# A two-layer graph network on one core: layer 0 gathers normalised rows instead of products, each edge group once

## The chip, the core and the metric

The kernel runs on one core of a Trainium2 chip. The metric is the device time of one execution in microseconds. Before the change the median of three runs is 3737.38 us (3736.8 to 3738.64).

## The reference, cut to what matters

x is 6250 x 512. There are 100,000 edges, sorted by destination. Layer 0 is a mean over neighbours with two weight matrices, layer 1 an attention over the same edges.

```
h = relu(layernorm(x))
agg = segment_sum(h[src], dst);  deg = number of edges into each node
z = relu(agg / max(deg, 1) @ W_l.T + b_l + h @ W_r.T)
x = x + batch_norm(z, gamma, beta)          # mean and variance over the nodes
h = relu(layernorm(x))
K, Q, V = h @ Wk, h @ Wq, h @ Wv
e = exp(clip(K[src] . Q[dst] / 8, -5, 5))   # for each of 8 heads
x = x + batch_norm(h + segment_sum(V[src] * e, dst) / segment_sum(e, dst))
```

## The kernel before

The nodes are cut into 49 windows of 128 rows (the last has 106), the edges into 391 groups of 256 (`GROUPS`; a group is G = 2 gathers of 128 rows). A step pairs one group with one window. A group whose edges run into the next window has one more step there, so there are 391 + 48 = 439 steps, padded to 440 (`STEPS`), in a loop of 55 passes of U = 8 steps each. Which window a step belongs to depends on the edges, so `prepare` makes tables of it on the chip, one number for each step: `win_t` the window, `col_t` its column in the tile `sums`, `par_t` which half of the PSUM tiles it uses, `new_t` whether it is the first step of a window. An engine reads an entry into a register with `load_values` (L927, the load itself is at L929) or `value_load`, and `If` branches on it.

Layer 0 has these stages, one after the other, each closed by a barrier of all engines:

- `prepare`: the tables, and for each step the 256 source rows (`src_t`) and places in the window (`rel_t`).
- `embed`: the weights are scaled, transposed and split into two float16 parts; then for each window the layer norm h (ScalarE, L704), its transpose (TensorE, L772), its high part (ScalarE, L709) and low part (VectorE, L650) into `slots`, which is the tile `sums` seen as float16, the product y = h W_l.T (TensorE, L781, 12 matmuls), its two parts (L715, L654) and their store to `y_d` (SP, L588). x comes in blocks of four windows through two buffers (SP, L583).
- `aggregate`: GpSimd issues the gathers of the rows of `y_d`, two for a step (L831), unrolled; rows outside the step's window have an index over the bound and aren't fetched. VectorE makes for each step the matrix `hot` (L848), 1 where a gathered row belongs to a row of the window. TensorE adds hot times rows into `pss` and counts into `psc` (L921, L923). At the first step of a window it also clears these (L901, L902) and puts the product h W_r.T into `psz` (L905, 12 matmuls). When a window has ended, VectorE flushes it (`flush`, L852): divides, adds, applies relu, stores into `sums` and adds up S1 and S2.
- `coefficients`, and then `dense`, `attend` and the last batch norm, which make layer 1.

The order on each engine is the order of the code; no planner is at work. On TensorE's queue a step of the gather loop is L908 to L925: two table entries, one branch, two waits, six matmuls. Semaphores: `rows_in[u]` counts landed gathers, `hot_made` and `ps_made` count steps of VectorE and TensorE; GpSimd refills a buffer when `ps_made` says that it has been read (L828).

Of the kernel before, what the change touches and what calls it, by code (L numbers as in the profile page):

```python
# [16 lines left out]
F32 = mybir.dt.float32  # L17
# [7 lines left out]
ds = bass.ds  # L25
# [6 lines left out]
def build(nc, x, src, dst, W_l, b_l, W_r, gamma0, beta0, Wq, Wk, Wv, gamma1, beta1, out):  # L32
# [25 lines left out]
    y_d = nc.dram_tensor("y_d", (WINDOWS * P, 2 * D), F16).ap()  # L58
# [18 lines left out]
    with life:  # L77
# [10 lines left out]
        early = ExitStack()  # L88
        win_t = sb(early, "win_t", [1, TS], I16)

# [16 lines left out]
        def prepare():  # L107
            with ExitStack() as ctx:
                fill = sb(ctx, "fill", [1, 2, TAIL], I32)
# [23 lines left out]
                ps_t = [pb(ctx, f"ps_t{k}", [P, 512]) for k in range(2)]  # L133

                filled, padded, got_first = sem("filled"), sem("padded"), sem("got_first")
# [7 lines left out]
                def _(block):  # L143
                    @block.sync
                    def _(sp):
                        sp.dma_start(first_i[:, :], dst[:].rearrange("(a e) -> a e", a=1)[:, 0:E:GE],
                                     allow_slow_non_contiguous=True).then_inc(got_first, 16)
                        for pad, given in ((src_pad, src), (dst_pad, dst)):
                            flat = pad.rearrange("a b -> (a b)")
                            sp.dma_start(flat[0:E].rearrange("(a b) -> a b", a=16),  # L150
                                         given[:].rearrange("(a b) -> a b", a=16)).then_inc(padded, 16)
                        sp.wait_ge(filled, 2)
                        for k, pad in enumerate((src_pad, dst_pad)):
                            flat = pad.rearrange("a b -> (a b)")
                            sp.dma_start(flat[E:E + TAIL].rearrange("(a b) -> a b", a=1),
                                         fill[:, k, :]).then_inc(padded, 16)

# [24 lines left out]
                    def _(pe):  # L182
# [11 lines left out]
                        last.then_inc(cols_ps, 1)  # L194
                        for n, (table, c) in enumerate((t, c) for t in range(2) for c in range(TCH)):
# [8 lines left out]
                            last.then_inc(turned, 1)  # L204

                    @block.vector
                    def _(dve):
# [33 lines left out]


# [9 lines left out]
                        for n, (table, c) in enumerate((t, c) for t in range(2) for c in range(TCH)):  # L252
# [3 lines left out]
                                                  ps_t[n % 2][:, 0:GE].rearrange("p (g s) -> p g s", g=G)).then_inc(stored, 1)  # L256

# [275 lines left out]
        def embed(w_r16, bias, unscale):  # L533

            with ExitStack() as ctx:
                w_l16 = sb(ctx, "w_l16", [P, 2, KC, D], F16)
                w_raw = sb(ctx, "w_raw", [P, 2, KC, D])
                big = sb(ctx, "big", [P, 2, KC])  # L540
                top = sb(ctx, "top", [P, KC])
                base2 = sb(ctx, "base2", [P, KC], I32)
                grow = sb(ctx, "grow", [P, KC])
                diag = sb(ctx, "diag", [P, KC, P])
                b_row = sb(ctx, "b_row", [1, D])
# [7 lines left out]
                y16 = sb(ctx, "y16", [P, 2, 2, D], F16)  # L553
                ps_w = [pb(ctx, f"ps_w{k}", [P, 512]) for k in range(2)]
                ps_u = pb(ctx, "ps_u", [P, 512])
                ps_b = pb(ctx, "ps_b0", [P, 512])
                ps_t = [pb(ctx, f"ps_t0{k}", [P, 512]) for k in range(2)]
                ps_o = [pb(ctx, f"ps_o0{k}", [P, 512]) for k in range(2)]
                w_in, b_in, x_in, stored = sems("w_in0", 2), sem("b_in0"), sems("x_in0", 2), sems("stored0", 2)
                chain, grown, w_scaled, w_turned, w_high, w_split, spread, unscaled = (  # L560
                    sem(n + "0") for n in ("wchain", "grown", "w_scaled", "w_turned", "w_high", "w_split", "spread", "unscaled"))
                counted, joined, var_ready, dev_ready, scale_ready, shift_ready = (
                    sem(n + "0") for n in ("counted", "joined", "var_ready", "dev_ready", "scale_ready", "shift_ready"))
                h_made, turned, high, split, made, y_high, y_low = (
                    sem(n + "0") for n in ("h_made", "turned", "high", "split", "made", "y_high", "y_low"))
                slots = sums[:, :].bitcast(F16)
                w16 = (w_l16, w_r16)
                assert FOURS % 2 == 0

                def slot(w, part):  # L570
                    return slots[:, ds(w * 2 * WIDTH + part * D, D)]
# [5 lines left out]
                def _(block):  # L577
                    @block.sync
                    def _(sp):
# [10 lines left out]
                        for k, w in enumerate((W_l, W_r)):  # L590
                            sp.dma_start(w_raw[:, k, :, :], w[:, :].rearrange("(c p) i -> p c i", p=P)).then_inc(w_in[k], 16)
                        load(0, 0)
                        sp.dma_start(b_row[:, :], b_l[:].rearrange("(a n) -> a n", a=1)).then_inc(b_in, 16)
                        load(1, 1)
                        with sp.Fori(0, FOURS // 2 - 1) as i:
                            for half in range(2):
                                for b in range(NB):
                                    store(NB * (2 * i + half) + b, b % 2)
                                load(2 * i + half + 2, half)
                        for b in range(NB):  # L600
                            store(NB * (FOURS - 2) + b, b % 2)
                        sp.wait_ge(h_made, NB * (FOURS - 1))
                        sp.dma_start(x_sb[0:LAST, 0, 0, :], x[(WINDOWS - 1) * P:N, :]).then_inc(x_in[0], 16)
                        for b in range(NB):
                            store(NB * (FOURS - 1) + b, b % 2)
                        store(WINDOWS - 1, 0)
                        for par in range(2):
# [822 lines left out]
```

## Time and profile before

| | |
|---|---|
| profiled execution | 3740.36 us |
| its span | 3738.0 us |
| median of the runs | 3737.38 us |
| `prepare`, from 0 us | 43.4 us |
| `embed`, from 43.4 us | 272.2 us |
| `aggregate`, from 315.6 us | 1174.4 us |
| the rest, from 1490 us | 2248.0 us |
| VectorE, TensorE, GpSimd busy in the span | 67%, 81%, 53% |

The stages don't overlap, so the span is the sum of the four, and what a change to one of them is worth shows in that stage alone. A queue's own instructions (register, branch, table entry) are not in an engine's busy time; the view by source line lists them with the letter q behind the engine: PEldq is TensorE's queue.

### The profile page before, as it was taken

What the parts mean: (1) busy time and instruction counts of PE and PEld (TensorE: products, weight loads), DVE (VectorE), ACT (ScalarE), POOL (GpSimd) and SP (SyncE); (2) the same over time, 40 slices, a digit from 0 to 9 for tenths busy, and PEclk for the clock granted to TensorE, in tenths of its full rate; (3) what the DMA queues carried; (4) which work ended last, traced back from release to release, by engine and by line L of the source; (5) the groups of instructions that cost most, each with busy time, mean ns of one, the idle gap of its engine ahead of it and who ended that gap; (6) DMA issues with size and microseconds to landing.
All of it is one profiled execution on the core that took longest, in us unless ns stands there. A gap on an engine that the chain in (4) does not pass through costs nothing. (4 is left out here: it accounts for less than half of the span.)

```text
span 3738.0 us, 59649 instructions
## 1 busy us (share of the span) xinstructions
PE 3025.4 (81%) x11648; PEld 1516.3 (41%) x11649; DVE 2503.8 (67%) x4615; ACT 1632.8 (44%) x6216; POOL 1991.4 (53%) x1929
## 2 busy tenths in 40 slices
PE   4776777777777776599998999999999999999640
PEld 2332222222222222488884444444444444444210
DVE  4444333333333333555557999999999999999999
ACT  2331000000000000222226999999999999999410
POOL 1004777777777776111115555555555555555455
PEclk9887766667776767799998999999999999999865
DMA  2334666666666665344446888887888888888337
GB/s 71 110 109 133 176 176 175 177 175 180 176 175 174 176 175 153 113 143 151 147 145 245 276 277 277 278 275 270 274 276 276 276 276 277 277 276 277 104 116 218
DMA packets 263476, 750.48 MB, mean 201 GB/s; under 512 B 54179, under 2 KB 54181, under 8 KB 263402
## 3 DMA queue, kind: packets, MB, share of 16 engines
q0 software_dynamic: 197504, 615.66, 52.1%
q1 hardware_dynamic: 58910, 121.60, 10.1%
q10 hardware_dynamic: 7020, 12.80, 0.9%
q14 instruction: 33, 0.27, 0.0%
q8 instruction: 9, 0.15, 0.0%
HBM read 750.45 MB, written 77.83 MB: 222 GB/s over the span
## 5 line engine op out<-in xcount | busy, mean ns | idle before, releaser
L1080 POOL DMA_INDIRECT kv<-kv_d,src_t x880 | 876.9, 997 | 633.4 <-PE psw L1226 464.1
L831 POOL DMA_INDIRECT rows<-y_d,src_t x880 | 898.0, 1020 | 555.8 <-DVE rows L838 288.1
L1102 ACT ACTIVATE kv<-kv,wgt 128x64 f32<-128x64 f32 x4400 | 1096.8, 334 | 0.0
L1223 PE MATMUL psa<-kv,hot 128*128 128x512 f32 x1760 | 863.6, 613 | 29.1 <-ACT kv L1102 27.7
L921 PE MATMUL pss<-rows,hot 128*128 128x512 f16 x1760 | 632.5, 494 | 273.4 <-DMA rows<-y_d,src_t 238.0
L1132 DVE TENSOR_TENSOR kv<-kv,ps_q 128x1024 f32<-128x1024 f32 x440 | 533.0, 1211 | 32.6 <-PE ps_q L1207 24.0
L1145 DVE TENSOR_REDUCE score<-kv 128x16 f32<-128x1024 f32 x440 | 531.2, 1207 | 0.0
L1019 ACT ACTIVATE var<-var 128x512 f32<-128x512 f32 x2 | 1.3, 629 | 1187.7 <-DVE var L1006 1187.7
L1223 PEld LDWEIGHTS psa<-kv,hot 128*128 128x128 f32 x1760 | 304.1, 190 | 395.9 <-issue 387.1
L1207 PE MATMUL ps_q<-sums,hotT 128*128 x1760 | 454.4, 381 | 0.1
L855 DVE TENSOR_SCALAR rd<-psc 128x1 f32 (+1 forms) x49 | 7.7, 158 | 599.7 <-PE psc L923 599.7
L921 PEld LDWEIGHTS pss<-rows,hot 128*128 128x128 f16 x1760 | 126.3, 109 | 497.5 <-issue 450.9
L1226 PE MATMUL psw<-parts,hot 128*128 128x16 f32 x880 | 302.2, 415 | 0.0
L848 DVE TENSOR_TENSOR hot<-lane,rel_t 128x256 f16<-128x256 f32 x440 | 187.9, 428 | 155.6 <-issue 97.2
L351 POOL TENSOR_TENSOR x_sb<-x_sb,C_bc 128x512 f32<-128x512 f32 x49 | 63.5, 1296 | 409.1 <-DMA x_sb<-in_x 409.1
L1226 PEld LDWEIGHTS psw<-parts,hot 128*128 128x128 f32 x880 | 167.8, 191 | 210.7 <-issue 210.7
L1138 DVE TENSOR_TENSOR kv<-kv,wgt 128x384 f32<-128x384 f32 x440 | 240.9, 547 | 0.3 <-ACT wgt L1095 0.3
L517 PE MATMUL ps_o<-w_hi,hT_hi 128*128 128x512 f32 x588 | 236.4, 402 | 0.0
L517 PE MATMUL ps_o<-w_lo,hT_hi 128*128 128x512 f32 x588 | 235.3, 400 | 0.0
L517 PE MATMUL ps_o<-w_hi,hT_lo 128*128 128x512 f32 x588 | 231.2, 393 | 0.0
L1207 PEld LDWEIGHTS ps_q<-sums,hotT 128*128 128x128 f16 x1760 | 172.4, 98 | 110.5 <-issue 2.0
L1198 PE MATMUL ps_h<-ident,hot 128*128 128x128 f32 x880 | 193.3, 302 | 14.9 <-DVE hot L1124 14.4
(191 smaller groups left out, 3620.1 us busy)
## 6 DMA issues: line engine op xcount, KB each, us to landing
kv_d<-o_sb SPq DMA_DIRECT2D x49, 512.0 KB, 2.8
rows<-y_d,src_t POOLq DMA_INDIRECT x880, 3.7
kv<-kv_d,src_t POOLq DMA_INDIRECT x880, 5.3
y_d<-y SPq DMA_DIRECT2D x49, 256.0 KB, 2.0
x_d<-x_sb SPq DMA_DIRECT2D x49, 256.0 KB, 3.2
h_d<-h SPq DMA_DIRECT2D x49, 256.0 KB, 3.4
h1b<-h_d SPq DMA_DIRECT2D x49, 256.0 KB, 2.7
x1b<-x_d SPq DMA_DIRECT2D x49, 256.0 KB, 4.0
```

What stands on the lines that cost most here:

```text
L517: last = nc.tensor.matmul(ps_o[par][k][:, :], a, b[:, k, c, :], start=(c == 0 and j == 0), stop=(c == KC - 1 and j == 2))
L831: pool.indirect_dma_start(rows[:, u, g, :], None, y_d[0:N, :], bass.IndirectOffsetOnAxis(src_t[:, m:m + 1], 0), bounds_check=limit, oob_is ...
L921: nc.tensor.matmul(pss[:, ds(par, D)], hot[:, u, g, :], rows[:, u, g, part * D:(part + 1) * D], start=False, stop=(g == G - 1 and part == ...
L1080: pool.indirect_dma_start(kv[:, u, g, :], None, kv_d[0:N, :], bass.IndirectOffsetOnAxis(src_t[:, m:m + 1], 0), bounds_check=limit, oob_is_ ...
L1102: last = nc.scalar.mul(v, v, wgt[:, u, g * HEADS + h:g * HEADS + h + 1])
L1132: nc.vector.tensor_tensor(k, k, ps_q[u % 2][:, :].rearrange("p (g d) -> p g d", g=G), ALU.mult).then_inc(multiplied, 1)
L1138: nc.vector.tensor_tensor(v, v, w.unsqueeze(3).to_broadcast([P, G, HEADS - HA, DH]), ALU.mult)
L1145: nc.vector.tensor_reduce(score[:, u, :].rearrange("p (g h) -> p g h", g=G), kv[:, u, :, 0:D].rearrange("p g (h d) -> p g h d", h=HEADS), ...
L1198: last = nc.tensor.transpose(ps_h[:, g * P:(g + 1) * P], hot[:, u, g, :].bitcast(F32), ident[:, :])
L1207: last = nc.tensor.matmul(ps_q[u % 2][:, g * D:(g + 1) * D], hotT[:, u % 2, g * P:(g + 1) * P], slots[:, ds(col * 2 + k * D, D)], start=(k ...
L1223: nc.tensor.matmul(pss[:, ds(par, D)], hot[:, u, g, :].bitcast(F32), kv[:, u, g, D:2 * D], start=False, stop=(g == G - 1), skip_group_chec ...
L1226: last = nc.tensor.matmul(psc[:, 0:2 * HEADS], hot[:, u, g, :], parts[:, u % 4, g, :, :].rearrange("p t h -> p (t h)"), start=False, stop= ...
```

## The change

- `embed` makes only h, and splits it without a transpose (ScalarE's high part straight from `h`, VectorE's low part too). TensorE has nothing to do there. The two parts are stored from `slots` to a tensor `h0_d` of the same shape as `y_d`. The next block of x is asked for after the third store of a block instead of the fourth. The work on the weights moves to `prepare`.
- `prepare` makes seven more tables (`end_t`, `done_t`, `past_t`, `prev_t`, `need_t`, `ring_t` for each step, `last_t` for each group) and the source rows in natural order, `nat_t`.
- In `aggregate` the gathers go by group, not by step: 391 x 2, without a bound, into a ring of 8 groups. TensorE reads from the tables where in the ring a step's group lies (`ring_t`) and how many groups must have landed (`need_t`). SP hands the landings on to TensorE (`ready`) and the buffers back to GpSimd (`free`).
- The sums in `pss` are now of h. After a window has ended, VectorE and ScalarE make its mean in two float16 parts (`average`, `turn_over`); TensorE transposes h (`turn_h`, in the next step), the mean (`turn_mean`, one step later) and makes both products (`multiply`, 24 matmuls, two steps later); VectorE flushes the window when the one after it ends. Before every step TensorE's queue tests for each of the three whether it is due.

```diff
+    then(nc.vector.memset(end_t[:, :], 0))
+    then(nc.vector.memset(done_t[:, 0:2], 0))
+    then(nc.vector.tensor_scalar(done_t[:, 2:TS + 2], win[:, :], -1.0, 0.0, ALU.add, ALU.max))
+    then(nc.vector.tensor_copy(end_t[:, 3:TS + 2], new_t[:, 1:TS]))
+    then(nc.vector.scalar_tensor_tensor(past_t[:, :], win[:, :], 2.0, new_t[:, :], ALU.is_ge, ALU.mult))
+    then(nc.vector.tensor_scalar(prev_t[:, :], win[:, :], -2.0, 0.0, ALU.add, ALU.max))
+    then(nc.vector.tensor_scalar(slot_i[:, :], grp[:, :], 0.0, float(GROUPS - 1), ALU.max, ALU.min))
+    then(nc.vector.tensor_scalar(need_t[:, :], slot_i[:, :], 1.0, None, ALU.add))
+    then(nc.vector.tensor_scalar(slot_i[:, :], slot_i[:, :], U - 1, None, ALU.bitwise_and))
+    then(nc.vector.tensor_scalar(ring_t[:, :], slot_i[:, :], float(G * 2 * D), None, ALU.mult))
+    dve.wait_ge(summed_g, 1)
+    then(nc.vector.scalar_tensor_tensor(last_t[:, 0:GROUPS], step[0:1, 0:GROUPS], float(U + 1), ps_g[0:1, 0:GROUPS],
+                                        ALU.add, ALU.add))
...
+        nc.vector.tensor_copy(nat_t[:, c * P:c * P + n], ps_t[c % 2][:, 0:n]).then_inc(stored, 1)
...
-    def store(w, par):
-        sp.wait_ge(y_high, w + 1)
-        sp.wait_ge(y_low, w + 1)
-        sp.dma_start(y_d[ds(w * P, P), :], y16[:, par, :, :].rearrange("p a d -> p (a d)")).then_inc(stored[par], 16)
+    def store(w):
+        sp.wait_ge(split, w + 1)
+        sp.dma_start(h0_d[ds(w * P, P), :], slot(w, 0, 2)).then_inc(stored, 16)
...
-            load(2 * i + half + 2, half)
+                    load(2 * i + half + 2, half)
...
+        nc.vector.tensor_tensor(slot(w, 1), h[:, b % 2, :], slot(w, 0), ALU.subtract).then_inc(split, 1)
...
+        act.wait_ge(h_made, w + 1)
+        nc.scalar.copy(slot(w, 0), h[:, b % 2, :]).then_inc(high, 1)
...
-    def products(w, par):
-        pe.wait_ge(split, w + 1)
-        if not below(w, 2):
-            pe.wait_ge(y_low, w - 1)
-        for c in range(KC):
-            for part, of in ((0, 0), (0, 1), (1, 0)):
-                last = nc.tensor.matmul(ps_o[par][:, :], slots[:, ds(w * 2 * WIDTH + part * D + c * P, P)], w_l16[:, of, c, :],
-                                        start=(c == 0 and part == of == 0), stop=(c == KC - 1 and part == 1))
...
-    limit = pool.alloc_register("limit0")
-    pool.reg_mov(limit, N - 1)
-    for s in range(STEPS):
-        u = s % U
-        if s < U:
-            pool.wait_ge(cleared, u + 1)
-        pool.wait_ge(ps_made, s + 1)
+    for n in range(GROUPS):
+        if n >= U:
+            pool.wait_ge(free, n - U + 1)
         for g in range(G):
-            m = s * G + g
-            pool.indirect_dma_start(rows[:, u, g, :], None, y_d[0:N, :],
-                                    bass.IndirectOffsetOnAxis(src_t[:, m:m + 1], 0),
-                                    bounds_check=limit, oob_is_err=False).then_inc(rows_in[u], 16)
+            pool.indirect_dma_start(at_ring(n % U, g), None, h0_d[0:N, :],
+                                    bass.IndirectOffsetOnAxis(nat_t[:, n * G + g:n * G + g + 1], 0)).then_inc(rows_in[n % U], 16)
+@block.sync
...
+    def pass_on(n, i, u, release=True):
+        sp.wait_ge(rows_in[u], 16 * G * (i + 1))
+        sp.sem_inc(ready, 1)
+        if release:
+            last = sp.value_load(last_t[0:1, ds(n - LAG, 1)], min_val=1, max_val=U + STEPS)
+            sp.wait_ge(ps_made, last)
+            sp.sem_inc(free, 1)
...
+    def turn_over(w, par):
+        act.wait_ge(rd_ready, w + 1)
+        nc.scalar.mul(mean[:, 0, :], pss[:, par * D:(par + 1) * D], rd[:, 0:1]).then_inc(mean_high, 1)
+        act.wait_ge(h_turned, w + 1)
+        act.wait_ge(products, w + 1)
+        for part in range(2):
+            last = nc.scalar.copy(hT[:, part, :], ps_x[part][:, :])
+        last.then_inc(h_copied, 1)
+        act.wait_ge(m_turned, w + 1)
+        for part in range(2):
+            last = nc.scalar.copy(mT[:, part, :], ps_x[part][:, :])
+        last.then_inc(m_copied, 1)
...
+    def average(w, par):
+        nc.vector.tensor_scalar(rd[:, :], psc[:, ds(par, 1)], 1.0, None, ALU.max).then_inc(counted, 1)
+        dve.wait_ge(counted, w + 1)
+        nc.vector.reciprocal(rd[:, :], rd[:, :]).then_inc(rd_ready, 1)
+        dve.wait_ge(mean_high, w + 1)
+        nc.vector.scalar_tensor_tensor(mean[:, 1, :], pss[:, ds(par, D)], rd[:, 0:1], mean[:, 0, :],
+                                       ALU.mult, ALU.subtract).then_inc(mean_split, 1)
...
+    def flush(w, n=P):
         base = w * IN_FLUSH
-        nc.vector.tensor_scalar(rd[:, :], psc[:, ds(par, 1)], 1.0, None, ALU.max).then_inc(flushing, 1)
+        to, kept = sums[:, ds(w * WIDTH, D)], sums[0:n, ds(w * WIDTH, D)]
+        dve.wait_ge(products, w + 2)
...
+    def close_before(s):
+        [ended] = load_values(mybir.EngineType.DVE, end_t, s + 2, 1, 1)
+        with dve.If(ended):
+            w = dve.value_load(win_t[0:1, ds(s - 1, 1)], min_val=0, max_val=WINDOWS - 1)
             [par] = load_values(mybir.EngineType.DVE, par_t, s - 1, 1, D)
-            w = dve.value_load(win_t[0:1, ds(s - 1, 1)], min_val=0, max_val=WINDOWS - 1)
+            [past] = load_values(mybir.EngineType.DVE, past_t, s, 1, 1)
+            with dve.If(past):
+                flush(dve.value_load(prev_t[0:1, ds(s, 1)], min_val=0, max_val=WINDOWS - 2))
             dve.wait_ge(ps_made, s + U)
             alone(dve)
-            flush(w, at, par)
...
-    def open_window(w, at, par):
-        pe.wait_ge(flushed, w + 1)
+    pe.sem_inc(products, 1)
+    pe.wait_ge(const, 2)
+    def turn(parts, count):
+        for part in range(2):
+            for c in range(KC):
+                last = nc.tensor.matmul(ps_x[part][:, c * P:(c + 1) * P], parts(part, c), ident16[:, :], start=True, stop=True)
+        last.then_inc(count, 1)
+    def turn_h(w):
+        pe.wait_ge(m_copied, w + 1)
+        turn(lambda part, c: slots[:, ds(w * 2 * WIDTH + part * D + c * P, P)], h_turned)
+    def turn_mean(w):
+        pe.wait_ge(h_copied, w + 1)
+        pe.wait_ge(mean_split, w + 3)
+        turn(lambda part, c: mean[:, part, c * P:(c + 1) * P], m_turned)
+    def multiply(w):
+        pe.wait_ge(m_copied, w + 2)
+        pe.wait_ge(taken, w + 1)
+        for k, (given, weights) in enumerate(((hT, w_r16), (mT, w_l16))):
+            for c in range(KC):
+                for part, of in ((0, 0), (0, 1), (1, 0)):
+                    last = nc.tensor.matmul(ps_z[:, :], given[:, part, c * P:(c + 1) * P], weights[:, of, c, :],
+                                            start=(k == c == part == of == 0), stop=(k == 1 and c == KC - 1 and part == 1))
+        last.then_inc(products, 1)
+    def of_window(s):
+        return pe.value_load(done_t[0:1, ds(s + 2, 1)], min_val=0, max_val=WINDOWS - 1)
+    def open_window(s, par):
+        w = pe.value_load(win_t[0:1, ds(s, 1)], min_val=0, max_val=WINDOWS - 1)
+        pe.wait_ge(mean_split, w + 1)
         nc.tensor.matmul(pss[:, ds(par, D)], zero[0:1, 0:P], zero[0:1, :], start=True, stop=False, skip_group_check=True)
         nc.tensor.matmul(psc[:, ds(par, 2)], zero[0:1, 0:P], zero[0:1, 0:2], start=True, stop=False, skip_group_check=True)
-        for c in range(KC):
-            for part, of in ((0, 0), (0, 1), (1, 0)):
-                nc.tensor.matmul(psz[:, ds(par, D)], slots[:, ds(at * 2 + part * D + c * P, P)], w_r16[:, of, c, :],
-                                 start=(c == 0 and part == of == 0), stop=(c == KC - 1 and part == 1), skip_group_check=True)
+    def after(s, lag, what):
+        [ended] = load_values(mybir.EngineType.PE, end_t, s - lag + 2, 1, 1)
+        with pe.If(ended):
+            what(of_window(s - lag))
     with pe.Fori(0, ITERS) as i:
         for u in range(U):
             s = i * U + u
+            after(s, 2, multiply)
+            after(s, 1, turn_mean)
+            after(s, 0, turn_h)
             [par] = load_values(mybir.EngineType.PE, par_t, s, 1, D)
             [new] = load_values(mybir.EngineType.PE, new_t, s, 1, 1)
+            [ring] = load_values(mybir.EngineType.PE, ring_t, s, 1, (U - 1) * G * 2 * D)
+            need = pe.value_load(need_t[0:1, ds(s, 1)], min_val=1, max_val=GROUPS)
             with pe.If(new):
-                [at] = load_values(mybir.EngineType.PE, col_t, s, 1, (WINDOWS - 1) * WIDTH)
-                w = pe.value_load(win_t[0:1, ds(s, 1)], min_val=0, max_val=WINDOWS - 1)
-                open_window(w, at, par)
+                open_window(s, par)
             pe.wait_ge(hot_made, s + 1)
-            pe.wait_ge(rows_in[u], (i + 1) * 16 * G)
+            pe.wait_ge(ready, need)
             for g in range(G):
                 for part in range(2):
-                    nc.tensor.matmul(pss[:, ds(par, D)], hot[:, u, g, :], rows[:, u, g, part * D:(part + 1) * D],
+                    nc.tensor.matmul(pss[:, ds(par, D)], hot[:, u, g, :], rows[:, ds(ring + (g * 2 + part) * D, D)],
                                      start=False, stop=(g == G - 1 and part == 1), skip_group_check=True)
                 last = nc.tensor.matmul(psc[:, ds(par, 2)], hot[:, u, g, :], ones16[:, :],
                                         start=False, stop=(g == G - 1), skip_group_check=True)
             last.then_inc(ps_made, 1)
+    after(STEPS, 2, multiply)
```

How the instructions stand, first TensorE's queue in the gather loop before the change, from the matmuls of one step to the branch of the next (L921 and L923 are matmuls, the lines at L929 load a table entry, L913 jumps over the opening of a window):

```order
L921 ISA
L921 MATMUL pss<-rows,hot 128x512 x2
L923 REGISTER_ALU
L923 MATMUL psc<-ones,hot 128x2
L921 MATMUL pss<-rows,hot 128x512 x2
L923 MATMUL psc<-ones,hot 128x2
L929 ISA
L929 TENSOR_LOAD par_t
L929 REGISTER_ALU
L929 TENSOR_LOAD new_t
L913 COMPARE_AND_BRANCH
```

Of the same place after the change, the first of the three tests ahead of a step, with what it jumps over (L1006 loads the entry, L973 is the branch, L958 the products):

```order
L994 MATMUL psc<-ones,hot 128x2
L1006 TENSOR_LOAD end_t
L973 COMPARE_AND_BRANCH
L963 REGISTER_ALU
L963 TENSOR_LOAD done_t
L963 ISA x2
L953 REGISTER_ALU
L954 REGISTER_ALU
L958 MATMUL ps_z<-w_r,hT 128x512 x12
L958 MATMUL ps_z<-w_l,mT 128x512 x12
L973 UNCONDITIONAL_BRANCH
```

It is followed by two more of this kind and then by the step's own four entries and the branch at L986 over the opening of a window (L1006 and L985 are entries, L992 the step's matmuls):

```order
L1006 REGISTER_ALU
L1006 TENSOR_LOAD par_t
L1006 REGISTER_ALU
L1006 TENSOR_LOAD new_t
L1006 REGISTER_ALU
L1006 TENSOR_LOAD ring_t
L985 REGISTER_ALU
L985 TENSOR_LOAD need_t
L985 ISA x2
L986 COMPARE_AND_BRANCH
```

The step's two entries have become four, three tests with an entry and a branch of their own stand ahead of them, and the 12 matmuls that stood in the opening have become 24 behind the first test.

GpSimd's queue from `prepare` to the end of `aggregate`, before:

```order
L177 DMA eidx<-dst_pad,grp_col 128x256
L102 UNCONDITIONAL_BRANCH
L820 UNCONDITIONAL_BRANCH
L831 DMA rows<-y_d,src_t 128x1024 x880
L102 UNCONDITIONAL_BRANCH
```

and after:

```order
L227 DMA eidx<-dst_pad,grp_col 128x256
L112 UNCONDITIONAL_BRANCH
L815 UNCONDITIONAL_BRANCH
L821 DMA rows<-h_d,nat_t 128x1024 x782
L112 UNCONDITIONAL_BRANCH
```

The gathers have become 782 instead of 880, and stand in the same place.

## Rows read from the trace of the kernel before

**Rows 1.** Stretches: length; PE, PEld, DVE, ACT, POOL busy (count); PEclk; DMA share; GB/s.
```profile
0.00:43.40 43.40, 11.98 (x36) 6.89 (x37) 17.37 (x47) 0.00 (x0) 10.11 (x21) 1.00 0.14 43
43.40:315.60 272.20, 188.03 (x826) 93.49 (x826) 125.40 (x257) 103.11 (x178) 0.00 (x0) 0.90 0.29 102
315.60:1490.00 1174.40, 858.84 (x3326) 325.55 (x3326) 395.11 (x843) 0.00 (x0) 898.02 (x880) 0.70 0.62 175
1490.00:3738.00 2248.00, 1966.58 (x7460) 1090.41 (x7460) 1965.95 (x3469) 1529.71 (x6038) 1083.23 (x1028) 0.94 0.69 229
```

**Rows 2.** Line L831, its instructions, its idle time, its landings.
```profile
L831 POOL DMA_INDIRECT rows<-y_d,src_t x880: 994/998/1520, 316.8 to 1481.8; - x176
...
  PE psc L923: 6.1, 20
...
DMA to landing us min/median/max: 2.1/3.7/4.4
```

**Rows 3.** Timeline near 1431 us: start, us, engine, line, tiles, idle before.
```profile
1430.52 1.00 POOL L831 DMA_INDIRECT rows<-y_d,src_t  x1 [0.30 <-issue]
...
1431.82 1.00 POOL L831 DMA_INDIRECT rows<-y_d,src_t  x1 [0.30 <-issue]
...
1433.29 1.03 PE L921 MATMUL pss<-rows,hot 128*128 128x512 f16 x2 [1.81 <-DMA rows<-y_d,src_t]
...
1434.19 1.01 PE L921 MATMUL pss<-rows,hot 128*128 128x512 f16 x2
```

**Rows 4.** PE queue, by source line: ns min/median/max, first and last start.
```profile
L929 PEldq ALU_OP  x489: 32/32/36, 316.3 to 1482.9; - x163
...
L929 PEldq TENSOR_LOAD <-par_t x440: 282/287/480, 315.8 to 1482.6; - x147
...
L929 PEldq FUSED_REGOPS  x385: 37/37/42, 326.0 to 1482.5; - x193
...
L913 PEldq COMPARE_BRANCH  x440: 66/207/369, 316.8 to 1483.4; - x147
...
L915 PEldq FUSED_REGOPS  x49: 151/151/168, 317.8 to 1466.2; - x49
...
L915 PEldq SEQ_ASSERT  x49: 18/18/32, 318.0 to 1466.4; - x49
...
L908 PEldq COMPARE_BRANCH  x55: 76/208/208, 340.7 to 1484.4; - x55
```

**Rows 5.** The same view of 1414.45 to 1420.4 us.
```profile
L929 PEldq FUSED_REGOPS  x3: 37/37/42, 1414.5 to 1420.2; - x3
...
L905 PEldq FUSED_REGOPS  x8: 46/46/65, 1417.0 to 1418.0; - x8
```

**Rows 6.** The page, DMA queues: packets, MB, share of 16 engines.
```profile
q14 instruction: 33, 0.27, 0.0%
```

**Rows 7.** Timeline of one block of four windows in `embed`.
```profile
220.45 0.69 DVE L632 BATCH_NORM_STATS2 st<-x_sb 128x6 f32<-128x512 f32 x1 [5.80 <-DMA x_sb<-in_x]
...
222.88 0.68 DVE L650 TENSOR_TENSOR sums<-ps_t,sums 128x512 f32 x1
...
229.72 0.58 ACT L709 CAST sums<-ps_t 128x512 f32 x1 [0.36 <-PE ps_t L772]
...
230.20 0.82 ACT L704 ACTIVATE h<-x_sb,nb,rs 128x512 f32<-128x512 f32 x1
...
234.31 0.41 SPq L583 DMA_DIRECT2D x_sb<-in_x  x1
...
239.99 0.69 DVE L632 BATCH_NORM_STATS2 st<-x_sb 128x6 f32<-128x512 f32 x1 [5.70 <-DMA x_sb<-in_x]
```

**Rows 8.** Timeline of `prepare` and of the weights.
```profile
31.29 0.35 DVE L245 TENSOR_SCALAR rel<-eidx,win_col 128x256 f32<-128x256 int32 x1 [13.11 <-DMA eidx<-dst_pad,grp_col]
...
49.05 2.29 DVE L621 TENSOR_REDUCE big<-w_raw 128x4 f32<-128x2048 f32 x1 [5.87 <-DMA w_raw<-in_L_gnn_W_l]
...
78.08 0.69 DVE L670 TENSOR_TENSOR bias<-bias,ps_b 128x512 f32<-128x512 f32 x1
```

More of the change, by code:

```diff
@@ L606, in _ @@
-                        store(WINDOWS - 1, 0)
-                        for par in range(2):
-                            sp.wait_ge(stored[par], 16 * (PAIRS + 1 - par))
+                            store(NB * (FOURS - 1) + b)
+                        store(WINDOWS - 1)
+                        sp.wait_ge(stored, 16 * WINDOWS)
                     @block.vector
                     def _(dve):
-                        done = [0]
-                        def then(ins):
-                            done[0] += 1
-                            ins.then_inc(chain, 1)
-                            dve.wait_ge(chain, done[0])
@@ new lines, in _ @@
+                    @block.sync
+                    def _(sp):
+                        LAG = U // 2
+                        def pass_on(n, i, u, release=True):
[5 more added lines that the diff above has]
+                                sp.sem_inc(free, 1)
+                        for u in range(U):
+                            pass_on(u, 0, u, u >= LAG)
+                        with sp.Fori(1, GROUPS // U) as i:
+                            for u in range(U):
+                                pass_on(i * U + u, i, u)
+                        for n in range(GROUPS // U * U, GROUPS):
+                            pass_on(n, n // U, n % U)
@@ new lines, in _ @@
+                    @block.scalar
+                    def _(act):
+                        act.sem_inc(m_copied, 1)
+                        nc.scalar.copy(ident16[:, :], ident[:, :]).then_inc(const, 1)
+                        def turn_over(w, par):
[10 more added lines that the diff above has]
+                            last.then_inc(m_copied, 1)
+                        with act.Fori(0, PAIRS) as i:
+                            for par in range(2):
+                                turn_over(2 * i + par, par)
+                        turn_over(WINDOWS - 1, 0)
@@ L925, in _ @@
                                 last.then_inc(ps_made, 1)
+                        after(STEPS, 2, multiply)
+                        after(STEPS, 1, turn_mean)
+                        after(STEPS + 1, 2, multiply)
+                        turn_h(WINDOWS - 1)
+                        turn_mean(WINDOWS - 1)
+                        multiply(WINDOWS - 1)
         def load_values(engine, table, s, n, most):
```

346 lines of the change are left out of this document (166 added, 180 removed).

## Prediction

> **What bounds the kernel now.** I read the stretches first. The stages follow one another, and the change touches the first three: 43.4, 272.2 and 1174.4 us [rows 1]. The 2248 us behind them keep their code and are carried over.
>
> In `aggregate` I then read the line of the gathers. The 880 gathers of L831 start from 316.8 to 1481.8 us, so one every 1.325 us, where one takes 0.998, and GpSimd waited for TensorE only 6.1 us in all [rows 2]. The timeline shows the same: 1.30 us from one gather to the next with 0.30 of issue between them, and TensorE waiting 1.81 us for rows to land [rows 3]. So GpSimd's queue sets the pace, 2.65 us for a step of two gathers. TensorE follows it at a mean granted clock of 0.70 with 859 us busy [rows 1].
>
> The third view is TensorE's own queue, which the busy time doesn't count. An entry of a table takes 0.287 us in it, a branch that jumps 0.207 us [rows 4], and a step has two entries and one branch. That this queue works one instruction after the other, also while the array is busy, is seen in 1414.5 to 1420.2 us: the three L929 instructions there enclose an opening of a window and one more step, without a wait for a landing [rows 5]. Counted off the listing these are 35 instructions. By the medians of [rows 4, 5] (four entries in the opening step and two in the other, 1.72; two branches, 0.28; the long L915 and its assert, 0.17; L905's eight, 0.39; the 17 others at 0.03 to 0.05, 0.63) they take 3.19 us; the stretch is 5.7 us. So behind each stand 0.07 us more, part of it for the 52 matmuls and weight loads pushed on the way. For the new step I take 0.065.
>
> In `embed` a block of four windows goes round in 19.5 us, from one landing of x (220.45) to the next (239.99): 13.9 us until the next load is issued at 234.31, and 5.7 until it lands [rows 7].
>
> **The change, part by part.** First the gathers. 782 at 1.325 are 1036 us instead of 1166, 130 less. What the bound check costs no row shows; at most the 0.33 us around the gather's own 0.998, so 780 to 1036, and I take 1036, the row of the same gather. This is worth something only as long as GpSimd sets the pace.
>
> TensorE's queue, ordinary step. In front of the step stand three entries and three branches that jump, then four entries, a long register instruction with its assert, and the branch over the opening; the six matmuls now need four address instructions, since the ring's place is a register. That makes 23 instructions: 7 entries at 0.286 (2.00), 4 jumps at 0.207 (0.83), 5 at 0.032 (0.16), 5 at 0.040 (0.20), 0.151 + 0.018 (0.17), sum 3.36; behind them 23 x 0.065 = 1.50. So 4.86 us, against 2.65 of the gathers. Even the recorded durations alone, 3.36, are longer than two gathers. 440 steps take 2138 us. The loop's end is a jump of 0.208 and two short ones, 0.5 us, 55 times: 27 us.
>
> The window's work. In 49 windows each of the four branches falls through once (0.07 instead of 0.21: -0.53) and each body loads one more number (0.032 + 0.286 + 0.151 + 0.018 + 4 x 0.065 = 0.75, four times 3.0). The other register instructions are seven short ones and nine for addresses, 1.7; pushing 80 more matmuls and weight loads I put at 0.2. So 4.4 us, 216 us in all.
>
> What lies beside it. TensorE's array has for two groups at the low clock 1.8 us (0.90 from one to the next [rows 3]), well below 4.86. The 24 matmuls of `multiply` take at most 24 x 0.45 = 10.8 us and are pushed in one go, while the queue reads the entries of the next two steps (9.7 us): hidden, at 1 to 5 us a window if not, 0 to 250 us; I take 0. VectorE's 395 us and ScalarE's three new copies and one scaling (about 0.6 us each by L709 [rows 7], five passes, 3 us of a window's 44) are beside it as well. The new waits: `turn_mean` stands one step, 4.9 us, behind the end of the window, and its mean is ready after about 2.5 us (two short VectorE instructions, under 0.35 each by L245 [rows 8], a ScalarE pass of 0.58 and a VectorE pass of 0.68 [rows 7], and their hand-overs); `multiply` one step later again. Behind a waiting instruction stand the next matmuls, and GpSimd waits behind those, but with 1.5 us or less of cover used up in 4.9, I take 0; with every wait a full 2.3 us it is 113. SP loads one entry for a group, 0.3 us of some 6: nothing.
>
> Ends of the stage: the first rows land 6 us after its start; behind the last step now stand the transposes, the mean, 24 matmuls at the low clock and the flush, 18 us. Sum of `aggregate`: 2138 + 27 + 216 + 24 = 2405 us instead of 1174.
>
> `embed` loses its products, so its round is the chain from landing to load. After a landing VectorE has two statistics (0.69 us, 0.9 with what joins them) and the low part of the first window (0.68); that frees ScalarE for the third (0.82 and 0.58); for the fourth it waits behind the square root until the fourth statistics, 5.4 us, and is done at 6.3. Then the load is issued and takes 5.7: 12.0 us for the round instead of 19.5. 12 rounds and 8 us of ends are 152 us instead of 272. With stores in the load's way up to 1 us more a round: 152 to 165.
>
> `prepare` takes over the weights, 49.05 to 78.77 us [rows 8], 29.7 us; it hides 13.1 us of them in the wait for `eidx` [rows 8]; the seven tables are 12 instructions of 512 numbers or fewer (0.4 us each, L245 has 0.35: 5 us), the natural order seven small transposes with their copies (I put 0.7 on each: 5 us). 43.4 + 29.7 - 13.1 + 10 = 70 us, 62 to 80.
>
> **The sum.** 70 + 152 + 2405 + 2248 = 4875 us of span, with the 2.4 us around it 4877; the profiled execution lay 3 us over the median, so 4874. I say 4870.
>
> **The rivals.**
>
> *GpSimd stays the bound* (faster). If the queue's entries were hidden behind the array, the stage would be 782 x 1.325 plus 30, 1066, and the time 70 + 152 + 1066 + 2248, 3539 us. For it: TensorE is 27% idle in this stage [rows 1]. Against: the steps of [rows 5] run at the queue's pace with the array full.
>
> *The array binds.* At the low clock 440 steps of 1.8, and 49 windows with 24 matmuls at 0.45, 16 transposes at about 0.12 and the opening's 1 us, are 792 + 672, 1464 us: 3940 us. This needs the queue to be hidden too, and a clock that doesn't rise under full load.
>
> *The loop's code is fetched anew in every pass.* The body grows from 530 to about 1240 instructions. If every piece of 128 (8 KB) cost 2 us when it is fetched, ten of them in 55 passes, 1100 us more: 5970. Against: only 33 pieces in the whole span [rows 6], with loop bodies of 500. The skill gives TensorE an instruction cache of 128 KB, four times that of the other engines (same page, ISA Cache), which would hold 1240 of 64 bytes; no run here shows it.
>
> *A jump costs no more than a branch that falls through.* The long ones of [rows 4] could be waits of another kind. At 0.07 (the minimum there) instead of 0.207 the four jumps of a step save 0.55 us, 241 us: 4630. Against: the median of 440 is the long one, 391 of them do jump. The Trainium skill speaks for less as well: "Advanced Engine Details and Errata", Control Flow Timing, states about 108 ns for a compare-and-branch; this trace doesn't agree (0.207), and by the page it would be about 4700 us.
>
> *The hand-overs at a window's end bite* (slower still): a wait of 2.3 us in the window and an unhidden `multiply` of 5 us, 7.3 x 49, 360 us: 5230.
>
> **How the numbers follow.** The forecast 0.77 (its own range 4650 to 5080: 4.4 to 5.3 us for a step), the hand-overs 0.07, the cheap jump 0.03, the refetch 0.04, GpSimd 0.04, the array 0.03, something else 0.02. My range leaves out the last five and takes in the unhidden `multiply` in part: 4650 to 5120. What a measurement can tell from no change is 0.2%, 7.5 us. Only the GpSimd case is faster, nothing that I can name lands within 0.2%, so 0.04, 0.01 and 0.95.
>
> **What would show it.** Right: in `aggregate` a step every 4.9 us, TensorE's seven entries and four branches following each other without a gap, an idle array with "issue" as its releaser, GpSimd waiting for SP, the DMA share at about half, granted clock mostly at the low level (0.5, 1.2 GHz); `embed` with a round of 12 us. Wrong: gathers at 1.3 us from one another, or waits of TensorE's queue for `ready`, `mean_split` or `m_copied`. A step under 4.4 us or over 5.3 means that the price of an entry, a jump, or of the gap behind them is not what I read.

## The result, and the profile after

The changed kernel takes 5060.86 us (median of 4 runs, 5059.87 to 5061.24), the kernel before 3738.01 us (4 runs, 3736.8 to 3742.25): a ratio of 1.3531, 95% interval 1.3514 to 1.3548. The forecast was 4870, in a range of 4650 to 5120. The direction and the mechanism came as said; the time is 190 us over the number.

The stretches of the profiled execution, cut at the same four places as before (columns as in [rows 1]):

```profile
0.00:65.40 65.40, 26.86 (x87) 16.78 (x88) 41.09 (x90) 10.76 (x17) 10.11 (x21) 0.86 0.21 67
65.40:233.40 168.00, 0.00 (x0) 0.00 (x0) 78.19 (x186) 71.45 (x112) 0.00 (x0) 0.50 0.45 153
233.40:2812.20 2578.80, 1250.59 (x4698) 518.36 (x4699) 387.50 (x835) 139.18 (x246) 758.12 (x782) 0.58 0.29 80
2812.20:5059.10 2246.90, 1961.12 (x7460) 1089.82 (x7460) 1969.16 (x3468) 1529.80 (x6038) 1086.81 (x1028) 0.95 0.68 230
```

`prepare` and `embed` together went from 316 to 233 us, `aggregate` from 1174 to 2579, and the rest stayed where it was. In `aggregate` the DMA share fell from 0.62 [rows 1] to 0.29, and the array is busy for less than half of the stretch.

The gathers, which set the pace before [rows 2], by their line (durations in ns, then idle time and how often):

```profile
L821 POOL DMA_INDIRECT rows<-h_d,nat_t x782: 940/946/1437, 234.2 to 2740.6; - x196
...
  SPq L834: 1625.3, 378
  POOLq L112: 205.3, 1
  issue: 123.9, 403
...
DMA to landing us min/median/max: 3.2/3.5/5.8
```

GpSimd now waits 1625 us for SP, which gives a place in the ring back only when TensorE has read it. Each gather is 52 ns shorter than with the bound (0.946 instead of 0.998), and that is worth nothing here.

The timeline of one ordinary step, where [rows 3] had TensorE waiting for rows:

```profile
1309.99 0.25 PEld L992 LDWEIGHTS pss<-rows,hot 128*128 128x128 f16 x2 [4.17 <-issue]
1310.00 1.03 PE L992 MATMUL pss<-rows,hot 128*128 x2 [3.69 <-issue]
...
1311.71 0.21 PE L994 MATMUL psc<-ones,hot 128*128 128x2 f16 x1
1312.23 0.94 POOL L821 DMA_INDIRECT rows<-h_d,nat_t  x1 [3.41 <-SPq L834]
1313.48 0.95 POOL L821 DMA_INDIRECT rows<-h_d,nat_t  x1 [0.30 <-issue]
1315.02 0.23 PEld L992 LDWEIGHTS pss<-rows,hot 128*128 128x128 f16 x2 [3.59 <-issue]
1315.03 1.03 PE L992 MATMUL pss<-rows,hot 128*128 x2 [3.11 <-issue]
```

From 1309.99 to 1315.02 is one step, 5.03 us, of which the array works 1.9 and then stands idle for 3.11 with "issue" as the releaser: nothing that the profile calls a wait. What fills that time is only in the view of the queue by source line (ns min/median/max, first and last start):

```profile
L1006 PEldq TENSOR_LOAD <-end_t x1323: 282/287/477, 234.2 to 2796.1; - x189
L1006 PEldq TENSOR_LOAD <-ring_t x440: 282/284/298, 237.6 to 2792.4; - x147
...
L985 PEldq TENSOR_LOAD <-need_t x440: 282/283/303, 238.1 to 2792.9; - x147
L985 PEldq FUSED_REGOPS  x440: 151/151/166, 238.4 to 2793.2; - x147
...
L973 PEldq COMPARE_BRANCH  x1323: 63/200/350, 234.7 to 2796.4; - x189
...
L986 PEldq COMPARE_BRANCH  x440: 75/207/217, 238.7 to 2793.5; - x147
...
L989 PEldq EVENT_SEMAPHORE  x440: 51/51/51, 240.0 to 2793.8; - x147
```

A step has seven entries and four branches, at the prices of [rows 4]. They follow one another with about 0.06 us between the end of one and the start of the next, 0.08 where matmuls are handed over in between. Of the 12,334 gaps of the stage 50 are over 1 us, and 48 of these stand behind L954 (below). Over the 439 distances between the L985 entries of one step and the next the shortest is 4.97 and the median 5.03 us.

### The profile page after: what moved, and what is told of

Same layout as the page of the kernel before. It is cut to its first block and busy times, and to the rows that moved or that the text cites. A ratio compares the mean times of both kernels' runs of the same rounds, so it can differ in the third digit from the quotient of the medians.

```text
span 5059.1 us, 70485 instructions
## 1 busy us (share of the span) xinstructions
PE 3238.6 (64%) x12245; PEld 1625.0 (32%) x12246; DVE 2475.9 (49%) x4579; ACT 1751.2 (35%) x6413; POOL 1855.0 (37%) x1831
## 5 line engine op out<-in xcount | busy, mean ns | idle before, releaser
L821 POOL DMA_INDIRECT rows<-h_d,nat_t x782 | 758.1, 969 | 1954.5 <-SPq L834 1625.3
L992 PE MATMUL pss<-rows,hot 128*128 x1760 | 776.6, 575 | 1083.3 <-issue 1020.4
L851 ACT ACTIVATE mean<-pss,rd 128x512 f16<-128x512 f32 x49 | 33.7, 687 | 2085.5 <-DVE rd L886 2085.5
L992 PEld LDWEIGHTS pss<-rows,hot 128*128 128x128 f16 x1760 | 161.6, 113 | 1367.9 <-issue 1343.4
L968 PE MATMUL pss<-zero 1*128 1x512 f32 x49 | 38.4, 784 | 311.7 <-issue 311.7
L958 PE MATMUL ps_z<-w_r,hT 128*128 128x512 f16 x588 | 207.7, 527 | 12.2 <-issue 10.3
```

Of the source, the lines that this page charges most:

```text
L821: pool.indirect_dma_start(at_ring(n % U, g), None, h0_d[0:N, :], bass.IndirectOffsetOnAxis(nat_t[:, n * G + g:n * G + g + 1], 0)).then_inc ...
L958: last = nc.tensor.matmul(ps_z[:, :], given[:, part, c * P:(c + 1) * P], weights[:, of, c, :], start=(k == c == part == of == 0), stop=(k ...
L992: nc.tensor.matmul(pss[:, ds(par, D)], hot[:, u, g, :], rows[:, ds(ring + (g * 2 + part) * D, D)], start=False, stop=(g == G - 1 and part ...
```

## The experiments

All are compared with the kernel before on the same chip. Stages are cut as above.

**Entries alone, not used.** In every step of the kernel before, ahead of its branch over the opening:

```diff
+    for _ in range(3):
+        load_values(mybir.EngineType.PE, nil_t, s, 1, 1)
```

> The kernel before, with three more table entries read by TensorE's queue in every step (values not used). My theory (the queue works one instruction after the other and is hidden only up to GpSimd's 2.65 us): an entry with the address instruction ahead of it takes 0.34 + 0.09 us, so 3 x 0.437 x 440 = 577 us more on the queue, whose own work without waits was 823 us in the stage; 1400 plus some 15 of ends, 1415 instead of 1174: 3980 us in all, with GpSimd waiting for TensorE. Rival (entries are hidden behind the array or prefetched): no change, 3740.

Measured 3741.17 us against 3740.79, ratio 1.0 (0.999 to 1.0009). This says nothing on either theory: the trace has no entry of `nil_t` on TensorE's queue, since a value that nobody reads is left out when the program is made. It shows only how well two programs agree that differ by one cleared table.

**Entries and jumps.**

```diff
+    for _ in range(3):
+        [nil] = load_values(mybir.EngineType.PE, nil_t, s, 1, 1)
+        with pe.If(nil):
+            pe.sem_inc(never, 1)
```

> The kernel before, with three more entries in every step and behind each a branch that always jumps (the table is all zero). My theory: each pair costs 0.437 + 0.265 us, 927 us more on the queue, stage 1765 us, 4330 in all, 350 over the run with the entries alone. Rival (a jump costs what a branch that falls through costs, 0.13 with its gap): 174 over the run with the entries alone, 4155. Rival (hidden): 3740.

Measured 4267.56 us (ratio 1.1403, 1.1384 to 1.1422). Its queue and its gathers:

```profile
L918 PEldq COMPARE_BRANCH  x1320: 200/200/337, 318.8 to 2012.3; - x189
...
L936 PEldq TENSOR_LOAD <-nil_t x1320: 281/283/324, 318.4 to 2012.0; - x189
...
L834 POOL DMA_INDIRECT rows<-y_d,src_t x880: 992/998/1231, 318.3 to 1985.6; - x176
...
  PE psc L930: 609.8, 305
```

GpSimd, which had waited 6.1 us for TensorE [rows 2], now waits 609.8. A step takes 3.51 us (median). Before it took 1.57 where nothing was waited for (the shortest distances between two L913 branches, 50 of 439 under 1.75 us), so 1.94 more: 3 x (0.344 + 0.259) with the gaps, and one address instruction of 0.093 for all three, where I had put one on each: that accounts for the 62 us by which the forecast was high. Entries hidden behind the array (3740) are out. Jumps at 0.13 would have made 3.1 us a step, so the cheap jump is out too.

**Entries that are used, and no jumps.**

```diff
+    nil = [load_values(mybir.EngineType.PE, nil_t, s, 1, 1)[0] for _ in range(6)]
+    count_at = sum(nil, par)
...
-    last = nc.tensor.matmul(psc[:, ds(par, 2)], hot[:, u, g, :], ones16[:, :],
+    last = nc.tensor.matmul(psc[:, ds(count_at, 2)], hot[:, u, g, :], ones16[:, :],
```

> The kernel before, with six more table entries (all zero) read by TensorE's queue in every step, and this time their sum goes into the address of the counts' matmuls, so that they can't be left out. No jumps. My theory: a step's queue had 1.57 us where nothing waited, and gets 6 x 0.344 + 0.09 us and about 0.1 for the sum: 3.8 us, over GpSimd's 2.65; with 118 us for the windows and 27 for the loop's ends 1817 us instead of 1174, 4380 in all. With the jumps' run (3.51 us a step) a jump is then worth 0.27 us with its gap. Rival (an entry is hidden, only jumps cost): 3740. Rival (an entry costs what a short register instruction does, 0.09): 3740 too, since the step stays at 2.2 us.

Measured 4443.04 us (ratio 1.1878, 1.1858 to 1.1898), 63 over the forecast.

```profile
L933 PEldq TENSOR_LOAD <-nil_t x2640: 281/288/310, 319.1 to 2188.5; - x189
...
L927 PEldq FUSED_REGOPS  x440: 175/175/186, 328.0 to 2189.4; - x147
```

A step takes 3.93 us (3.8 expected), 2.36 more: 6 x 0.346, 0.093, and 0.14 for the longer address instruction of L927, and 0.05 over that sum. An entry is thus paid in full, and from the run before 1.94 - 0.093 - 3 x 0.344 leaves three jumps at 0.27 us each with their gaps. The rival of a cheap jump had 0.13 with its gap.

**One test ahead of the three.** The changed kernel with a table `due_t`, the largest of the three entries that are tested:

```diff
+    [due] = load_values(mybir.EngineType.PE, due_t, s, 1, 1)
+    with pe.If(due):
+        after(s, 2, multiply)
+        after(s, 1, turn_mean)
+        after(s, 0, turn_h)
-    after(s, 2, multiply)
-    after(s, 1, turn_mean)
-    after(s, 0, turn_h)
```

> The changed kernel with one test more ahead of the three (a table that says whether any of them is due), so that an ordinary step has five entries and two jumps instead of seven and four. My theory (the number of queue instructions sets the step): 1.40 us less in some 293 steps, 0.57 more in some 147: ordinary step 3.6 us instead of 5.0, 326 us less, 4735. Rival (it is the fetching of the loop's code, which grows here): no less than 5060. Rival (hand-overs at a window's end make the rest): less than 200 us won.

Measured 4859.12 us (ratio 1.2985, 1.2963 to 1.3007), 202 under the changed kernel's 5060.86: more than nothing, which refutes the fetch, but 124 less than I had said. It is also hardly more than the 200 that the rival of the hand-overs allowed, so by its total alone this run doesn't tell that rival from the queue; the steps do. An ordinary step takes 3.92 us and not 3.6: two entries and two jumps went (1.22 us), but one more register instruction came (0.10), since the wait is now computed on its own, and none of the tests' address instructions went, since the three tests had shared one. A step in which h or the mean is turned went up from 6.74 to 7.64 us, 0.9 instead of 0.57, because values that were read ahead of the branch are made anew behind it.

**Eight matmuls for a window instead of 24.** The 16 matmuls that have a low part in them are left out:

```diff
-    for part, of in ((0, 0), (0, 1), (1, 0)):
-        last = nc.tensor.matmul(ps_z[:, :], given[:, part, c * P:(c + 1) * P], weights[:, of, c, :],
+    last = nc.tensor.matmul(ps_z[:, :], given[:, 0, c * P:(c + 1) * P], weights[:, 0, c, :],
...
```

> The changed kernel with 8 instead of 24 matmuls in the products of a window (only high part times high part; the other 16 are left out). The trace shows 2.61 us between the last register instruction ahead of these matmuls and the next entry. Theory A (each of the 48 matmuls and weight loads takes 0.054 us to hand over): 0.9 us instead of 2.6, 85 us less, 4975. Theory B (handing over is cheap, the queue to the array is full and waits for it): 0.1 to 0.25 us, 112 to 120 us less, 4945. Rival (the gap is a fetch of code, which is there whatever the matmuls are): no less than 5050, the gap stays at 2 us or more.

Measured 4947.54 us (ratio 1.3221, 1.3199 to 1.3243), 113 less. In the changed kernel the last register instruction ahead of the products and the first entry behind them stand like this (the view of the queue, 344.5 to 348.5 us, for the entry to 347.6):

```profile
L954 PEldq ALU_OP  x1: 32/32/32, 344.8 to 344.8; - x1
...
L1006 PEldq TENSOR_LOAD <-end_t x1: 286/286/286, 347.5 to 347.5; - x1
```

and in this kernel at the same kind of place:

```profile
L954 PEldq ALU_OP  x1: 32/32/32, 292.7 to 292.7; - x1
...
L1005 PEldq TENSOR_LOAD <-end_t x2: 283/285/287, 292.8 to 293.5; - x2
```

The median gap over all 48 windows is 2.61 us in the one and 0.08 in the other; the mean is 2.45 in the changed kernel, and 48 x (2.45 - 0.08) is 114 us, the whole difference. Theory A, 0.054 us for each matmul and load, would have left 0.9 us here; so 8 matmuls and 8 weight loads are handed over for next to nothing, and with 24 and 24 the queue stands. Theory B, that it waits until the array has taken some, is the one that fits, and the trace of the changed kernel shows how many (the timeline, 344.5 to 348.5 us):

```profile
344.93 0.13 PEld L958 LDWEIGHTS ps_z<-w_r,hT 128*128 128x128 f16 x2 [1.16 <-issue]
...
347.04 0.15 PEld L958 LDWEIGHTS ps_z<-w_r,hT 128*128 128x128 f16 x1 [0.28 <-issue]
347.47 0.15 PEld L958 LDWEIGHTS ps_z<-w_r,hT 128*128 128x128 f16 x1 [0.28 <-issue]
347.83 0.74 PEld L958 LDWEIGHTS ps_z<-w_r,hT 128*128 128x128 f16 x4 [0.21 <-issue]
```

When the next entry starts, at 347.49, the array has begun 8 of the 24 loads and 7 of the 24 matmuls, and 33 of the 48 lie handed over and not begun. It is 8 and 7 in all 48 windows, and the same in the four other runs that have these 24 matmuls; only the time that the array takes for them differs (1.86 to 2.61 us here). With 8 and 8 at most 16 are handed over at this place.

The page's instruction line is the same in both kernels, and in all the kernels with the new stage:

```profile
q14 instruction: 297, 2.43, 0.2%
```

264 pieces more than [rows 6] do come, but their number doesn't move when TensorE's loop loses 256 instructions (this run) or more, and no gap of TensorE's queue is left that they could explain. In the changed kernel they come with the windows and not with the passes of TensorE's loop: from 12 us before to 2 us behind each L954 the DMA packets have five of them in 41 of 48 cases. Whose code they are no run shows.

**By step instead of natural order.** The changed kernel with this part undone: `ring_t`, `need_t` and SP's handing on go, the 880 gathers with a bound come back.

```diff
-    [ring] = load_values(mybir.EngineType.PE, ring_t, s, 1, (U - 1) * G * 2 * D)
-    need = pe.value_load(need_t[0:1, ds(s, 1)], min_val=1, max_val=GROUPS)
...
-    pe.wait_ge(ready, need)
+    pe.wait_ge(rows_in[u], (i + 1) * 16 * G)
```

> The changed kernel with the gathers of the kernel before in place of the natural order: 880 by step, with a bound, each step its own place; the entries for the place in the ring and for the count of groups go, and SP hands nothing on. The three tests and the rest of the change stay. My theory (the queue's instructions): five entries, four jumps and seven short ones, 3.4 us a step instead of 5.03, still over GpSimd's 2.65: 440 x 3.4 + 320 for the windows + 27 + 18 of ends, 1860 us for the stage, 4340 in all, so the natural order cost some 700 us of the 1320. Rival (the natural order was worth its 130 us on GpSimd): over 5060. Rival (only the tests' jumps count): 4900 or more.

Measured 4348.2 us (ratio 1.1625, 1.1606 to 1.1644); a step takes 3.44 us. So the natural order, whose own row promised 130 us, costs 713: two entries, the asserted load's long register instruction with its assert, three address instructions for places that are no longer fixed, and two short ones, nine of 24 instructions and 1.58 us of a step.

```profile
L826 POOL DMA_INDIRECT rows<-h_d,src_t x880: 992/997/1462, 237.0 to 2051.3; - x176
...
  PE psc L980: 772.0, 383
```

GpSimd still waits 772 us for TensorE, this time because of the tests.

**All look-ups in one number, gathers by step.** Half of the sums and three flags in one 16-bit entry; the work at a window's end stays as changed.

```diff
+    [v] = load_values(mybir.EngineType.PE, pack_t, s, 1, D + 7)
+    par = v & D
+    with pe.If(v & 7):
+        with pe.If(v & 4):
+            multiply(of_window(s - 2))
+        with pe.If(v & 2):
+            turn_mean(of_window(s - 1))
+        with pe.If(v & 1):
+            w = of_window(s)
+            turn_h(w)
+            open_window(w + 1, par)
```

> The changed kernel with the gathers of the kernel before (880, by step, with a bound, each with its own place, so neither a place in the ring nor a count of groups is looked up) and with half of the sums and the three tests in one number for each step: one entry, one jump over everything that a window's end needs. New embed and both products at the window's end stay. Theory A (the queue's time is the sum of its instructions): by the slots of the runs so far an ordinary step is 1.33 us of queue, a window's work 9.0 us more, 1053 us in all, under GpSimd's 1166; GpSimd sets the pace again: 65 + 168 + 1190 + 2247 = 3670 us, 2% faster than before. Rival (the array binds: at the low clock a window of nine steps has 16.2 + 10.2 + 3 = 29 us of matmuls against 23.8 of gathers): 49 x 29.4 = 1440, 3920 us. Between them, if the clock rises for a part of the time as before: 3700 to 3800.

Measured 3668.19 us (5 runs, 3665.63 to 3670.21; ratio 0.9806, 0.9793 to 0.982): 1.9% under the kernel before, and as forecast (3670). Its `embed` and `aggregate`, columns as above:

```profile
61.50:232.60 171.10, 2.67 (x11) 1.19 (x9) 81.19 (x193) 71.75 (x113) 0.00 (x0) 1.00 0.45 150
232.60:1419.30 1186.70, 945.70 (x4698) 431.22 (x4698) 396.04 (x843) 138.36 (x245) 898.89 (x880) 0.83 0.63 175
```

and its gathers, by their line:

```profile
L814 POOL DMA_INDIRECT rows<-h_d,src_t x880: 994/999/1522, 233.4 to 1399.2; - x176
...
  PE psc L972: 20.1, 66
```

The shortest steps take 1.33 us, as summed from the slots. GpSimd is the bound again (20.1 us of waits for TensorE, and 1.33 us from one gather to the next, as before), although the window's products are all in this stage. The stage is no shorter for it: 1187 us against 1174. The 72 us that this kernel gains over the one before come from `embed`, 171 us instead of 272, less 18 us more in `prepare` (61.5) and 12 more in `aggregate`. The array didn't bind either: its granted clock is 0.83 here, between the levels of 1.2 and 2.4 GHz, where the changed kernel with the same 4698 matmuls had 0.58, near the low one, and they took 946 us busy instead of 1251. What the array did ahead of it differs in that it had less idle time. So the rival that the array binds, 3920 us, is out.

**All look-ups in one number, natural order.** The same with the group's number in a 32-bit entry as well:

```diff
+    par = v & D
+    ring = v & (U - 1) * G * 2 * D
+    need = (v >> 11) + 1
```

> The changed kernel with everything that a step looks up (half of the sums, place in the ring, count of groups, three tests) in one 32-bit number: one entry and one jump for an ordinary step instead of seven and four, but more register instructions. Gathers, ring and handing on as changed. Theory A (sum of the slots): an ordinary step 2.17 us, a window's work 9.0 us, 27 for the loop's ends: 1420 us for the stage with its ends, 65 + 168 + 1420 + 2247 = 3900. Rival (the number of groups binds, GpSimd at 1.27 us for a gather): 993 + 25, 3500. Rival (the seven entries did not matter, what binds is the hand-overs at a window's end): over 4600.

Measured 3881.59 us (ratio 1.037, 1.0354 to 1.0386), with 1397.5 us for the stage (1420 expected) and 2.12 us for the median step (2.17). GpSimd waits 402 us for SP. Six entries and three jumps fewer in a step, with the gathers, the ring and the window's matmuls as they were, take away 1179 us of the 1323 that the changed kernel lies over before; that refutes the hand-overs at a window's end as the cause.

## Why the prediction was right, and where the 190 us are

By its own steps, on the profiled execution (5059.1 us of span against 4875):

| step | predicted | measured |
|---|---|---|
| `prepare` | 70 | 65.4 |
| `embed` | 152 | 168.0 |
| ordinary steps (440) | 2138 | 2218 |
| loop's ends | 27 | 27 |
| window's extra (49) | 216 | 321 |
| ends of `aggregate` | 24 | 13 |
| the rest | 2248 | 2246.9 |

The measured parts of `aggregate` are sums over the queue's instructions, each from its start to the start of the next: 2566 us in all. The window's extra is what stands on the lines of its work (L940 to L969), 347 us, less 26 that the branches which fall through save. The ordinary steps are what is left of the 2566.

- *The bound* moved from GpSimd to TensorE's queue, as said. The two runs on the kernel before show that entries and jumps do it by themselves; the one with the gathers by step and the packed ones take it back.
- *The ordinary step* was 5.04 us on average, 4.86 predicted. I counted 23 instructions and left out the wait (L989, 0.106 with its gap). The 256 steps that have just these 24 instructions take 5.02 us: 3.45 of durations, where the sum had 3.36, and 24 gaps of 0.065 each, as taken. Of the 0.09 in the durations 0.05 is the wait's own, and the rest is that the short register instructions last up to 0.06 and not 0.03 to 0.04. The last 0.02 lies in the steps with a window's work. Together 80 us.
- *The window's extra* is the term that was mis-sized: 105 us. The step said that the 24 matmuls are "pushed in one go" while the queue goes on, and put 0.2 us on it, with 0 to 250 us for `multiply` unhidden, of which it took 0. The trace has 2.45 us on average between L954 and the next entry, and the run with eight matmuls takes 113 us away, nearly all of it. It was inside the bounds, and the value taken was the wrong one: the array's work does lie beside the queue's, but only what the queue has been able to hand over, here 33 matmuls and loads.
- *`embed`*: its round is 13.3 us, 12.0 predicted, 12 rounds are the 16 us. The load goes out 7.1 us after the landing, 6.3 predicted, and takes 6.1 us, 5.7 predicted. The last of its block's rows has been read at 122.92, 6.5 us after the landing, but SP is then issuing the store that stands ahead of the load in its queue, up to 123.34. The prediction had such stores as a case of its own, 152 to 165 us; the stage came out 3 over that:

```profile
116.44 0.69 DVE L706 BATCH_NORM_STATS2 st<-x_sb 128x6 f32<-128x512 f32 x1 [5.39 <-DMA x_sb<-in_x]
...
122.12 0.80 ACT L759 ACTIVATE h<-x_sb,nb,rs 128x512 f32<-128x512 f32 x1
...
123.57 0.40 SPq L679 DMA_DIRECT2D x_sb<-in_x  x1
...
129.70 0.69 DVE L706 BATCH_NORM_STATS2 st<-x_sb 128x6 f32<-128x512 f32 x1 [4.80 <-DMA x_sb<-in_x]
```

- *`prepare` and the ends* came out 5 and 11 us shorter than said, which hides a little of the rest.
- *The rivals.* GpSimd as the bound needed 3539 us (its four parts add up to 3536): in the changed kernel it waits for SP for 1625 us. The array: busy for 1251 of the stage's 2579 us. The code fetched anew: more pieces, no time. The cheap jump: 0.27 us with its gap, and the 1320 branches that were added to the kernel before, which all jump, last 200 ns or more each. The Trainium skill, "Advanced Engine Details and Errata", Control Flow Timing, has about 108 ns for a compare-and-branch; the branches that jump don't show it in any run here (medians of 200 and 207 ns). The hand-overs: TensorE's waits for `m_copied`, `h_copied` and `mean_split` leave no gap over 0.15 us in its queue but for two behind the last step, and the array begins the products 0.05 us behind L954 in all 48 windows, so they don't wait for `m_copied` there either.

## What to carry to other kernels

Count what the queue of the slowest engine has to do in a step, at the price of a table entry (0.34 us) and a jump (0.27), before adding a test or a look-up: a conditional that hardly ever holds costs its entry and its jump every time. Put everything that a step looks up into one number and one branch over all the rare work; here, with fixed places for the rows, that took the stage from 2579 us to 1187. It only brought the stage back to the gathers' pace: the 72 us under the kernel before come from `embed`. And a transfer saved is worth something only while transfers set the pace: the natural order saved 98 gathers and cost 713 us.

## What the runs showed that I had not expected

- Eight matmuls with their weight loads leave 0.08 us of gap in TensorE's queue, 24 with theirs 2.61 us. The queue goes on when 33 of the 48 are still to be begun, in every window.
- A gather without a bound takes 0.946 us on GpSimd, one with a bound 0.998.
- The same 4698 matmuls are busy for 1251 us at a granted clock of 0.58, 1140 at 0.67 (gathers by step), 1032 at 0.77 (packed, natural order) and 946 at 0.83 (packed, by step). Over these four the clock rose as the stage got shorter, from 2579 to 1865, 1398 and 1187 us; but the run with one test ahead, 2374 us, has 0.58 and 1282 us busy, no better than the longest.
